# One stream of 78 expert tiles per layer, a new wait on GpSimd, and two batches gathered and combined later

## What is computed

```python
x = x + linear_and_block_cumsum(layernorm(x))      # W 128x128, cumsum over each row of 128
x = x + ffn(layernorm(x))
x = x + attention(layernorm(x))                    # 16 heads of 8, keys j with i-128 <= j <= i
x = x + ffn(layernorm(x))

def ffn(x):                                        # E = 8 experts, K = 2, D = 128, H = 512
    xn = layernorm(x) * gamma + beta
    w, idx = top_k(softmax((xn @ router_w.T) / 1.5), 2)
    h = silu(xn @ W1[e]); y = h @ W2[e]            # only the two chosen experts count
    return sum over the two of w * y, + x
```

## Time and profile before

| | us |
|---|---|
| median of 3 runs (983.61 to 986.66) | 985.13 |
| the profiled execution | 979.9 |
| its span, first to last instruction | 977.8 |
| PE busy (70%) | 684.0 |
| DVE busy (62%) | 611.0 |
| POOL busy (45%) | 435.3 |
| ACT busy (42%) | 408.3 |

### The profile page before, as it was taken

How to read it: one execution, slowest core, us unless ns; L and a number is a source line. 1 busy time by engine, 2 the same in 40 slices (tenths; PEclk the granted TensorE clock), 3 DMA queues, 4 the chain that set the end, 5 groups by cost and what they waited for, 6 DMA issues and landing times.

```text
span 977.8 us, 30500 instructions
## 1 busy us (share of the span) xinstructions
PE 684.0 (70%) x11616; PEld 523.8 (54%) x11616; DVE 611.0 (62%) x1840; ACT 408.3 (42%) x691; POOL 435.3 (45%) x409
## 2 busy tenths in 40 slices
PE   3811767797657677988888988877576777566770
PEld 2511556575545554655655656655375556455560
DVE  7888797854454557656656565677678544354444
ACT  1370245353333342754654655655354334233340
POOL 6591573484655600112122100050576766666661
PEclk9999977999988899999998999967767988798886
DMA  7210012132222221221211201001021111233114
GB/s 221 68 33 0 25 23 81 48 64 56 65 56 76 72 73 36 62 61 30 72 46 45 70 26 36 6 19 28 17 69 39 44 45 39 66 83 102 56 39 137
DMA packets 62923, 54.61 MB, mean 56 GB/s; under 512 B 10129, under 2 KB 55954, under 8 KB 62778
## 3 DMA queue, kind: packets, MB, share of 16 engines
q1 hardware_dynamic: 53250, 33.12, 11.8%
q0 software_dynamic: 9536, 19.55, 8.0%
HBM read 31.79 MB, written 20.84 MB: 54 GB/s over the span
## 4 chain that ended last, share of the span: by engine, by line
PE 43%; DVE 29%; issue 12%; another core or an unknown queue 6%; DVEq 4%; ACT 3%; DMA 2%; POOL 1%; SPq 0%; ACTq 0%; POOLq 0%
PE stbank L1109 6%; PE bank L1212 4%; PE stbank L1096 4%; PE sbank L1170 3%; DVE gl L767 3%; PE stbank L1110 3%; PE stbank L1098 3%; DVE zr L586 3%; DVE mx L825 2%; PE sbank L1165 2%; PE stbank L1196 2%; PE stbank L1097 2%; DVE ysb L757 2%; DVE xs L783 2%
## 5 line engine op out<-in xcount | busy, mean ns | idle before, releaser
L478 POOL DMA_INDIRECT xg<-table,idx x156 | 159.1, 1020 | 162.8 <-PE sbank L1077 66.4
L903 ACT ACTIVATE g<-stbank 128x512 f32<-128x512 f32 x156 | 93.3, 598 | 316.1 <-PE stbank L1098 242.5
L1109 PE MATMUL stbank<-wff,gh 128*128 x624 | 142.3, 306 | 112.0 <-DVE ysb L757 74.5
L757 DVE TENSOR_REDUCE ysb<-stbank 128x128 f32<-128x256 f32 x156 | 65.9, 423 | 152.4 <-remote 88.5
L1096 PE MATMUL stbank<-xT,wff 128*128 128x128 f16 x624 | 148.8, 246 | 17.3 <-issue 9.7
L825 DVE TENSOR_REDUCE mx<-sbank 128x2 f32<-128x320 f32 (+1 forms) x256 | 116.1, 472 | 68.6 <-PE sbank L1170 61.4
L950 ACT ACTIVATE pT<-stbank 128x1024 f32<-128x1024 f32 (+1 forms) x128 | 116.8, 917 | 81.4 <-PE stbank L1196 80.2
L1098 PE MATMUL stbank<-xT,wff 128*128 128x128 f16 x624 | 149.1, 246 | 0.0
L1097 PE MATMUL stbank<-xT,wff 128*128 128x128 f16 x624 | 146.5, 242 | 0.0
L1109 PEld LDWEIGHTS stbank<-wff,gh 128*128 128x128 f16 x624 | 67.5, 108 | 144.3 <-issue 126.6
L1110 PE MATMUL stbank<-wff,gl 128*128 x624 | 130.2, 239 | 0.0
(11 more groups left out here) (188 smaller groups left out, 1334.0 us busy)
## 6 DMA issues: line engine op xcount, KB each, us to landing
yslot<-ysb SPq DMA_DIRECT2D x78, 64.0 KB
table<-tb SPq DMA_DIRECT2D x16, 256.0 KB
cg<-ytab SPq DMA_DIRECT2D x16, 256.0 KB
qz<-dumps SPq DMA_DIRECT2D x96, 32.0 KB
kst<-dumps SPq DMA_DIRECT2D x96, 32.0 KB
xg<-table,idx POOLq DMA_INDIRECT x156
xs<-in_x SPq DMA_DIRECT2D x8, 256.0 KB, 4.6
qz<-in_w SPq DMA_DIRECT2D x1, 2048.0 KB, 10.4
```

What stands on the lines that cost most here:

```text
L478: g.indirect_dma_start(xg[:, i % G].rearrange("p a d -> p (a d)"), None, table[cc % 2], bass.IndirectOffsetOnAxis(ap=idx[:, cc % 2, t:t + ...
L903: a.activation(g32[:, i % 3, :], hbank[i % 2], ACT.Silu, scale=1.0 / WSCALE)
L1109: mm(o, gh[:, i % 3, P * f:P * f + P], whl, start=(f == 0), stop=False, skip_group_check=True)
```

## The change

1. Per layer one stream of 78 tiles in 88 steps (`layer_tile` maps a step to a tile, its chunk and its place in it). The second chunk's first tile follows the first chunk's last one in the next step. What stood beside the second chunk's steps still stands at steps 44 to 87, where tiles 44 to 77 are now transposed. The waits for the second chunk's table and indices stand at its first tile.
2. `tile_under_way`: GpSimd's second transfer of a step (the gather back in layer 0, the scatter in layer 1) first waits for the hidden product of tile s-3.
3. `BACK_EARLY` = 2: beside the stream only batches 0 and 1 are gathered back and combined. Batch 2 is gathered while the first batch is scored, each gather after a unit of scoring, and combined between its last units; batch 3 is gathered and combined during the first batch's products, by the same code as batches 4 to 7.

```diff
+BACK_EARLY = 2
+        def layer_tile(layer, n):
+
+            i = tile_of(CHUNKS * layer, n)
+            return (i, i // SLOT_TILES, i % SLOT_TILES) if 0 <= n < CHUNKS * SLOT_TILES else (None, None, None)
...
         def gathered_back_at(s):
-            return s - BACK_AT if 0 <= s - BACK_AT < BPC * GATHERS else None
+            return s - BACK_AT if 0 <= s - BACK_AT < BACK_EARLY * GATHERS else None
...
             c0 = CHUNKS * layer
-            for s in range(XSTEPS):
-                x_step(c0, s)
-                if layer == 0:
+            for s in range(2 * XSTEPS):
+                x_step(layer, s)
+                if s >= XSTEPS:
+                    beside(layer, s - XSTEPS)
+                elif layer == 0:
                     a_step(1, s)
                     r_step(c0 + 1, s - A_BEFORE_R)
                 else:
                     r_step(c0 + 1, s)
-            for s in range(XSTEPS):
-                x_step(c0 + 1, s)
-                beside(layer, s)
...
+            def tile_under_way(layer, s):
+
+                i, _, _ = layer_tile(layer, s - 3)
+                if i is not None:
+                    pool.wait_ge(s_h, i + 1)
+
...
-                for t in (s - 6,) if s < XSTEPS - 1 else (s - 6, s - 5):
-                    if cc >= CHUNKS and t >= 0:
-                        i = tile_of(cc, t)
-                        pool.wait_ge(s_yc, i + 1)
-                        g.indirect_dma_start(ytab[cc % 2], bass.IndirectOffsetOnAxis(ap=sidx[:, cc % 2, t:t + 1], axis=0),
-                                             ysb[:, i % G, :], None).then_inc(s_sc[i % G], 16)
+                for n in range(AHEAD + 1) if s == 0 else (s + AHEAD,):
+                    i, cc, t = layer_tile(layer, n)
+                    if i is None:
+                        continue
+                    if t == 0:
+                        pool.wait_ge(s_idx, cc + 1)
+                        for k in range(2):
+                            pool.wait_ge(s_tbd[k], 16 * 2 * (cc + 1))
+                    wait(pool, s_xp, i - G + 1)
+                    g.indirect_dma_start(xg[:, i % G].rearrange("p a d -> p (a d)"), None, table[cc % 2],
+                                         bass.IndirectOffsetOnAxis(ap=idx[:, cc % 2, t:t + 1], axis=0)).then_inc(s_g[i % G], 16)
+
+                i, cc, t = layer_tile(layer, s - 6)
+                if layer and i is not None:
+                    tile_under_way(layer, s)
+                    pool.wait_ge(s_yc, i + 1)
+                    g.indirect_dma_start(ytab[cc % 2], bass.IndirectOffsetOnAxis(ap=sidx[:, cc % 2, t:t + 1], axis=0),
+                                         ysb[:, i % G, :], None).then_inc(s_sc[i % G], 16)
...
                 if layer == 0 and m is not None:
+                    tile_under_way(layer, XSTEPS + s)
                     gather_back(m // GATHERS, m % GATHERS)
...
+            for m in range(GATHERS):
+                wait(pool, s_red, 2 * m)
+                gather_back(2, m)
             front(2, 2)
+            for m in range(2):
+                gather_back(3, m)
             for b in range(B):
                 for j in range(UNITS):
-                    if BPC <= b + 4 < B and j in (UNITS - 3, UNITS - 1):
+                    if BACK_EARLY <= b + 4 < B and j in (UNITS - 3, UNITS - 1):
...
-                    if BPC <= b + 3 < B and j % 2 == 0 and j // 2 + 2 < GATHERS:
+                    if BACK_EARLY <= b + 3 < B and j % 2 == 0 and j // 2 + 2 < GATHERS:
...
                 if j in (0, 1):
-                    if b >= BPC:
+                    if b >= BACK_EARLY:
                         combine(0, b, j)
...
             for j in range(UNITS):
                 reduce(0, j)
-                if j in (MAX_AT, UNITS - 1):
-                    front(2, 2 if j == MAX_AT else 3)
+                if j >= MAX_AT:
+                    front(2, j - MAX_AT)
```

More of the change, by code:

```diff
@@ L225, in combined_at @@
             b = s - BACK_AT - GATHERS - 1
-            return b // GATHERS if b >= 0 and b % GATHERS == 0 and b // GATHERS < BPC else None
+            return b // GATHERS if b >= 0 and b % GATHERS == 0 and b // GATHERS < BACK_EARLY else None
         def prepared_at(s):
@@ L295, in r_step, with x_step @@
                                  tb[:, i % 2].rearrange("p t a d -> p t (a d)")).then_inc(s_tbd[i % 2], 16)
-            def x_step(cc, s):
-                t = s - 5
-                if cc < CHUNKS and t >= 0:
-                    i = tile_of(cc, t)
+            def x_step(layer, s):
+                i, cc, t = layer_tile(layer, s - 5)
+                if layer == 0 and i is not None:
                     sp.wait_ge(s_yc, i + 1)
@@ L747, in r_step, with x_step @@
                     v.tensor_tensor(sidx[:, cp, :], row, far, ALU.add).then_inc(s_idx, 1)
-            def x_step(cc, s):
-                if 0 <= s - 5 < SLOT_TILES:
-                    i = tile_of(cc, s - 5)
+            def x_step(layer, s):
+                i, _, _ = layer_tile(layer, s - 5)
+                if i is not None:
                     dve.wait_ge(s_y, i + 1)
@@ L757, in x_step @@
                     v.tensor_reduce(ysb[:, i % G, :], ybank.rearrange("p (a d) -> p d a", a=2), AX.X, ALU.add).then_inc(s_yc, 1)
-                if s < SLOT_TILES:
-                    i = tile_of(cc, s)
+                i, _, _ = layer_tile(layer, s)
+                if i is not None:
                     dve.wait_ge(s_xp, i + 1)
@@ L762, in x_step @@
                     v.tensor_copy(xT[:, i % 3, :], xbank[i % 2]).then_inc(s_xt, 1)
-                if 0 <= s - 3 < SLOT_TILES:
-                    i = tile_of(cc, s - 3)
+                i, _, _ = layer_tile(layer, s - 3)
+                if i is not None:
                     dve.wait_ge(s_gh, i + 1)
@@ L895, in r_step, with x_step @@
                     split_high((k - 6) // 2)
-            def x_step(cc, s):
-                if 0 <= s - 2 < SLOT_TILES:
-                    i = tile_of(cc, s - 2)
+            def x_step(layer, s):
+                i, _, _ = layer_tile(layer, s - 2)
+                if i is not None:
                     act.wait_ge(s_h, i + 1)
@@ L1078, in x_step @@
                     ins.then_inc(s_xp, 1)
-                if s % LOADS == 0 and s < SLOT_TILES:
-                    n = min(LOADS, SLOT_TILES - s)
-                    _, ids = nc.values_load_multi_w_load_instructions(
-                        eid[0:1, cc % 2, s:s + n], [mybir.EngineType.PE], min_val=0, max_val=E - 1,
-                        skip_runtime_bounds_check_because="a count of thresholds passed, cut off at E - 1")
-                    for k in range(n):
-                        experts[s + k] = wff[:, bass.ds(ids[k], 1), :, :]
-                if 0 <= s - 2 < SLOT_TILES:
-                    i = tile_of(cc, s - 2)
+                    if t % LOADS == 0:
+                        n = min(LOADS, SLOT_TILES - t)
+                        _, ids = nc.values_load_multi_w_load_instructions(
+                            eid[0:1, cc % 2, t:t + n], [mybir.EngineType.PE], min_val=0, max_val=E - 1,
+                            skip_runtime_bounds_check_because="a count of thresholds passed, cut off at E - 1")
+                        for k in range(n):
+                            experts[i + k] = wff[:, bass.ds(ids[k], 1), :, :]
+                i, _, _ = layer_tile(layer, s - 2)
+                if i is not None:
                     pe.wait_ge(s_xt, i + 1)
@@ L1099, in x_step @@
                     ins.then_inc(s_h, 1)
-                if 0 <= s - 4 < SLOT_TILES:
-                    i = tile_of(cc, s - 4)
+                i, _, _ = layer_tile(layer, s - 4)
+                if i is not None:
                     pe.wait_ge(s_gl, i + 1)
```

31 lines of the change are left out of this document (10 added, 21 removed).

## The result

The changed kernel took 976.2 us (median of ten runs, 972.8 to 981.8) beside 984.9 of the kernel before (ten runs, 980.5 to 987.0). The ratio is 0.9922, with a 95% interval from 0.9898 to 0.9946: 0.8% faster. Forecast were 961.5 and 2.4%.

A forecast was written before the change was run, and what follows sets the result against it. TensorE and VectorE alternate on the chain, and TensorE's completions are seen late while GpSimd issues transfers back to back. Terms -21 + 2.3 + 1.1 + 3 - 3 - 6 = -23.6 from 979.9, plus 5.2, give 961.5 us; 8-in-10 range 944 to 983.

The forecast's parts named there:

- Layer 0's stream: Layer 0: one stream with sixteen fewer second transfers ends the stage at 344.9, a gain of 21 us (bounds 0 and 36).
- Batch 2's combination: First batch's scoring: two half combinations of 1.14 us between VectorE's reductions, covered by nothing, +2.3 us.
- Scoring's gathers: First batch's scoring: batch 2's gathers, issued back to back, may hold TensorE's completions, +3 us (between 0 and 7).
- Batch 3's part: First batch's products: batch 3's combination moved there, 0.88 of it on the chain, +1.1 us (between 0 and 2.3).
- Layer 1's boundary: Layer 1's chunk boundary: the pause goes, ten tiles take 30.2 us instead of 33.2, -3.0 (bounds 0 and -14).
- The new wait: Second transfers, both layers: GpSimd stops one transfer earlier when completions are held, -6 us (bounds -42 and +51).
- the wait does nothing: Rival on the second transfers' wait: holds come from elsewhere or it is always satisfied; 967.5 us, chance 0.15.
- The saved transfers don't show: Rival on layer 0's second half: projections, not gathers, set its pace of 3.78, scoring's gathers hold fully; 986.5 us, chance 0.07.
- The rival on the slower side: Both layers' second transfers: the wait stops GpSimd after every pair, 3.6 us a tile; 1018 us, chance 0.08.

The follow-up runs named there:

- e15: Changed kernel without the new wait of the second transfer, on a chip with late completions: 0.9925 of the kernel before.
- e16: Changed kernel with batch 2's gathers beside the stream, its combination still in scoring, on a chip with late completions: 0.992 of the kernel before.
- e1: Changed kernel without the new wait, on a chip without late completions: 0.9992 of the kernel before.
- e6: The changed kernel itself, timed again on a chip without late completions: 0.9988 of the kernel before.
- e9: Changed kernel with gathers back from step 1 and projections from step 9, on a chip with late completions: 0.9926 of the kernel before.
- e10: As e9, with all four batches gathered and combined beside the stream, same chip: 0.9897 of the kernel before.
- e4: Changed kernel with batch 2's gathers beside the stream, its combination still in scoring, on a chip without late completions: 0.9998 of the kernel before.
- e13: Changed kernel with batch 2's eight gathers in one go behind the last tile gather, on a chip without late completions: 0.999 of the kernel before.
- e5: The kernel before, unchanged, profiled on a chip without late completions: 908.5 us in its one run.
- e14: The kernel of e10 without the new wait, on a chip without late completions: 0.9952 of the kernel before.
- e7: The kernel before with the new wait alone added, on a chip without late completions: 0.9998 of the kernel before.
- e11: The kernel of e1 once more, on another chip without late completions: 1.0002 of the kernel before.
- e17: The kernel of e14 on a chip with late completions: 971.1 us, 0.9923 of the kernel before.
- e18: The kernel of e10, with the new wait, on the same chip as e17: 966.0 us, 0.9874 of the kernel before.

## Why the prediction was wrong

The direction was right and so was the reading of what bounds the kernel; the size was not. By its own terms, on the profiled executions:

- **Layer 0's stream, -21.** The tiles ended 19.8 us sooner. But this term had scoring start near 345, and it started at 352.1. I had given what is left of the projections 2.3 us. In fact the stream ends five steps sooner and its company doesn't: behind the last tile the chain runs through batch 1's last products (L1154), the copy (L947) and the masks (L1269), at half clock in this profile. The gap grew by 3.7 us; at full clock (e15 and e16 on a late chip, e1, e6 and others on the first kind) by 2.3, with TensorE's first scoring waiting for the last stack transfers (`kst<-dumps`) in e6 and e15. e9 and e10, with that company five steps earlier, have 1.9 again: shown.

```profile
346.46 1.83 PE bank L1154 x8
348.29 0.02 issue
348.31 0.79 ACT vp L947 x4
349.11 0.04 issue
349.15 0.59 PE bank L1159 x2
349.74 1.73 PE stbank L1269 x4
```

- **Batch 2's combination, +2.3.** e16 and e4 have 21.2 us of scoring against 18.8 to 19.9 without it: 1.3 to 2.4. Right.
- **Scoring's gathers, +3.** The first step that failed, by its size: 29.1 against 21.2 in e15 and e16, 7.9 us, above my bound of 7. I had counted a pause of one microsecond for about half of seven gathers. The holds came to some 5 us by the estimate above. The clock, which I had put at nothing without a reason, adds 2.6: TensorE fell to the lower level among the gathers and had it back only in part in the stage's last 10 us (0.74).
- **Batch 3's part, +1.1.** Measured +6.0, and 43.4 against 34.8 between e9 and e10. I priced the combination alone from the earlier trace rows and held the gathers harmless because the exponentials pace them. Four of them go out in a row around the stage's start (368.2 to 373.0 in e16), and again the clock falls (0.50 between 372 and 380 there); how the 6.0 splits between holds and clock no run shows. On the chips without late completions first products take 35.2 to 38.4 us with the part in them (e13, e4) and 34.7 to 35.4 without (e5, e14), at most 3.7 more.
- **Layer 1's boundary, -3.** From the first reduction to that of the first tile behind the boundary it took 129.5 us before and 126.5 now: -3.0. Right for those tiles. But the sum put the tiles right behind them at nothing: the six reductions after that first one took 17.0 us before, when their gathers had gone out without scatters between them, and take 18.6 now (12.6 and 15.3 in e5 and e6). Layer 1 as a whole gained 2.2, and 1.3 in e6.
- **The new wait, -6.** The second step that failed: no gain in e1, e7, e11 and e15. GpSimd's idle time before the scatter now does end with the hidden product, seen late or not (line 1115 is its last matmul):

```profile
L496 POOL DMA_INDIRECT ytab<-ysb,sidx x78 | 78.8, 1011 | 48.6 <-remote 20.1 <-issue 15.4 <-PE stbank L1115 11.3
```

  But I had placed 69 of the 85 waits in layer 1, and there they give nothing: layer 1 takes 233.0 us without and 232.4 with the wait on E (e15, e16), 231.5 and 232.4 on F (e17, e18). The runs of transfers did become a little shorter, as I had it: counted as transfers less than 0.45 us apart, layer 1 has 17 runs of three and 18 of four in the changed kernel and 26 of four in e15. But the number of stops stayed the same (48 runs and 46), and so did the pace. In layer 0 e18 shows a gain of 4.8 us from 32 waits. At that price, an estimate, the changed kernel's 16 would give 2.4, less than the comparison of two chips can tell. So the term's size in e18 (5.1 for 6) agrees with my -6 by luck: the number of waits and their place are others.

The errors of these terms are 5.4 for the start of scoring (15.6 us gained instead of 21), 4.9 for the gathers, 4.9 for batch 3's part and 6, together some 21; the profiled executions differ by 3.3 us where 23.6 was forecast. The medians differ by 8.7, since the profiled run of before lay 5.0 below its median and that of the changed kernel 0.4 above its own.

Of the rivals, "the wait does nothing" was right about the changed kernel's wait, as far as the runs can tell, and wrong about why, since completions are late on such a chip. The Trainium skill ("SBUF — State Buffer", section "SBUF: two separate sides") says that among the engines' ports to SBUF only the pair that VectorE and GpSimd share is contended, and that TensorE never waits on anyone. My prediction stretched this to the time at which TensorE's completions are seen. On A, B and D the traces agree even with that: no start is put down to "remote" in any of them. On the other chips they don't: the same program has 88.5 us of late starts behind TensorE before one instruction, and taking eight transfers out of scoring shortens that stage by 7.9 us. No run here looks at a port, so the page's own sentence is neither shown nor refuted.

"The saved transfers don't show" is in its outcome, not in its reason, what the chips of the first kind do: layer 0 gains 5.4 us there, since nothing was held at the second transfers, and the whole change is worth 0.1% with an interval around nothing. The rival on the slower side did not happen anywhere.

What stays open: why some chips show TensorE's completions late behind GpSimd's transfers and others don't; how the wait shortens layer 0 with 32 second transfers and why it does nothing in layer 1. No run separates the late completion itself from the lower clock in first products.

## What to carry to other kernels

Work that is moved into a stage where two engines alternate step by step can cost far more than its own time: on a late chip eight gathers cost such a stage 7.9 us, most of it as a stall of both engines and 2.6 us, by an estimate, through the lower clock. On the other chips the same gathers cost it nothing, and there only VectorE's own part (1.6 us) showed. When a stream is shortened, ask what stood beside its last steps. And a cause that is read from one chip's trace should be looked at on a second chip before a change is built on it: this change is worth 0.8% on one kind and nothing on the other.

## What the hardware showed that was not expected

- The kernel before takes 912 to 914 us on three chips and 978 to 985 on the three others and in the first pair. Of the 71 us between its two profiles (979.9 and e5's 908.5) 28.5 lie in layer 0, 31.6 in layer 1 and 12.0 between first products and layer 1's first tile. Layer 0's first chunk, with one transfer per tile, takes 112 us in both, first tile to last. Single gathers take nearly the same (means of 1.01 to 1.05 us over both kinds).
- TensorE's granted clock went from 1.00 to 0.50 within scoring once the same matmuls came with waits between them (e15), and stayed at 1.00 without (e16). Where TensorE and VectorE alternate, half the clock alone cost little: 4.7 us instead of 3.8 for eight reductions.
